# Overflow groups of 64 tokens, two to a tile, in an audio tower's tree feed-forward; the static residual moved next to its scatter

## The chip, the cores and the metric

The kernel runs on one core of one Trainium2 chip, in one launch. The metric is the device time of the launch in microseconds. The profile comes from one more execution, whose own time is given beside its span.

## What is computed

The input is four sequences of 750 x 128. A three-tap convolution of signs (64 features out) and a normalisation give h, 748 tokens a sequence, 2992 tokens in all. An attention of 8 heads, of which only the diagonal weight of each token is used, is added to h. Then comes the part that the change touches, a tree of 255 nodes with 128 leaves:

```python
current = zeros(T)                                  # T = 2992 tokens, all at the root
for _ in range(8):
    score = einsum('td,td->t', flat_x, w1s[current]) + b1s[current]
    choice = ((sign(score) + 1) / 2)
    current = current * 2 + choice + 1              # left or right child
path_weights = gelu(abs(logits))                    # 8 per token
for i in range(8):
    t_i = einsum('td,tdo->to', flat_x, w2s[nodes_i]) + b2s[nodes_i]
    out = out + t_i * path_weights[:, i]            # 64 x 64 matrix of each node on the path
h = h + out
```

Each token thus needs eight 64 x 64 matrices, and which eight depends on its leaf alone. How many tokens a leaf has is known only when the kernel runs.

## The kernel before

Five engines run their own instruction streams; semaphores order them. The work falls into two stages.

**Attention and routing (until about 360 us).** 16 units, each one pair of heads of one sequence, of 12 score tiles of 125 x 748. TensorE forms a tile (L964), VectorE takes its negated maxima (L1438), ScalarE the exponentials with their sums (L1238). Three PSUM tensors of 1024 columns take turns. Ahead of unit w, SP copies the high and low halves of q and k into stacks in SBUF: eight DMAs, four at L389 and four at L395, which unit w of TensorE waits for (`scores`, L961). SP issues all of these, the table loads and the zero fill in one order. The zero fill (L410) stands after the copies of w = 5: one DMA that writes a row of zeros, with a token number out of range, to every slot of the table `sorted_rows`, `F_TILES` x 128 slots of 130 floats. Later fills of the attention work compute each token's leaf, its rank in the leaf and its slot; GpSimd scatters the tokens' rows (normalised x, a one, h, token number) into their slots (L668).

**The tree (from 361.8 us).** A leaf has 32 static slots (`G`): tile k of 32 static tiles holds leaves 4k to 4k + 3. Tokens beyond 32 go to overflow groups of 32, four groups to a tile, at most `OVG` = 96 groups. A section is four tiles; SP loads its rows in one DMA (`load_rows`, six buffers `xs`), TensorE transposes them (`xs_T`, L1046), ScalarE copies that (`xs_copy`, L1303).

- Static tile: TensorE multiplies with fixed slices of the tables (L1066 to L1073); ScalarE computes the gates (L1310, L1312) and weighs the first four levels (L1321), VectorE the other four (L1730) and sums the eight levels (L1738) into one of `NO` = 12 buffers `yo`. GpSimd adds the residual (`residual`, L742) and scatters the 128 rows to the output (`rows_out`, L750). The loop issues residual k + 1 ahead of scatter k.
- Overflow tile: the leaf numbers of a tile's four groups are packed in one register, 7 bits each; of these TensorE computes the addresses. For each group four products with the group's 32 columns of the transposed rows as the stationary operand: 195, 130, 65 and 65 columns (L1096 to L1102), into one bank for each group (`OWN`); then one product of the whole tile with the root's matrix (L1108). ScalarE copies the four groups (L1342) and the root (L1344) to `yv` in SBUF, computes the gates; VectorE weighs all levels (L1727), sums (L1738) and adds the residual (L1744); GpSimd only scatters. Group g of the next tile waits until the copy of group g is out of its bank. `yv` and the weighted values have two buffers each.

The number of groups is loaded into a register on each engine. Each of the six sections is unrolled and stands in an `If` of its own, one behind the other. SP waits at the end for every scatter (L453, L457). SP's `load_rows(k)` from the seventh on waits until the tiles that had its buffer are scattered. VectorE's sum of tile k waits for the scatter of tile k - 12.

Of the kernel before, what the change touches and what calls it, by code (L numbers as in the profile page):

```python
# [11 lines left out]
DEPTH = 8  # L12
NODES = 2 ** DEPTH - 1
LEAVES = 2 ** (DEPTH - 1)
P = 128
# [24 lines left out]
G = 32  # L40
OVG = 96
STAT = LEAVES * G
SLOTS = STAT + OVG * G
ST_TILES, OV_TILES = STAT // P, OVG * G // P
# [18 lines left out]
def tower(nc, x, k_tok, bias, beta, mean, var, Wqkv, bqkv, W0, b0, w1s, b1s, w2s, b2s, rows, hbuf, out):  # L63
# [6 lines left out]
    with ctx:  # L70
# [114 lines left out]
        EARLY = 12  # L185
# [6 lines left out]
        def banks(k):  # L192

            return k + 4 * max(0, k - ST_TILES)
# [139 lines left out]
        def _(sp):  # L334
# [113 lines left out]
            for k in range(ST_TILES // 4, F_TILES // 4 - 1):  # L448
                with sp.If(groups > 4 * (4 * k - ST_TILES)):
                    load_rows(k + 1)  # L450
# [3 lines left out]
            for m in range(ST_TILES // 4, F_TILES // 4):  # L454
                with sp.If(groups > 4 * (4 * m - ST_TILES)):
                    for k in range(4 * m, 4 * m + 4):
                        sp.wait_ge(s_outr[k % NO], 16 * (k // NO + 1))  # L457

        @block.gpsimd
        def _(pool):  # L460
# [297 lines left out]
            for m in range(ST_TILES // 4, F_TILES // 4):  # L758
                with pool.If(groups > 4 * (4 * m - ST_TILES)):  # L759
                    for k in range(4 * m, 4 * m + 4):  # L760
                        rows_out(k)

        @block.tensor
        def _(pe):
# [312 lines left out]
            def load_leaves(k):  # L1077

                kk = k - ST_TILES
                return nc.tensor.value_load(lam4[0:1, kk:kk + 1], min_val=0, max_val=LEAVES ** 4 - 1)  # L1080

            def overflow_products(k, leaves):
# [4 lines left out]
                for g in range(4):  # L1087
                    if n:
                        pe.wait_ge(s_yv, 4 * (n - 1) + g + 1)
                    elif g % 2 == 0:  # L1090
                        bank_ready(ST_TILES + g // 2)
                    y = OWN[g][0:G]
                    xg = xk[:, G * g:G * (g + 1)]
                    own = leaves >> 7 * g if g else leaves
                    leaf = nc.tensor.snap(own & LEAVES - 1 if g < 3 else own)
# [15 lines left out]
            early = [load_leaves(k) for k in range(ST_TILES, ST_TILES + EARLY)]  # L1111
# [10 lines left out]
            for m in range(ST_TILES // 4, F_TILES // 4):  # L1122
                with pe.If(groups > 4 * (4 * m - ST_TILES)):
                    for k in range(4 * m, 4 * m + 4):
                        n = k - ST_TILES
                        overflow_products(k, early[n] if n < EARLY else load_leaves(k))
                        if k % 4 == 1 and k + 4 < F_TILES:
                            xs_T(m + 1)

        @block.scalar  # L1130
        def _(act):
# [202 lines left out]
            for m in range(ST_TILES // 4, F_TILES // 4):  # L1334
                with act.If(groups > 4 * (4 * m - ST_TILES)):
                    for k in range(4 * m, 4 * m + 4):
                        if k >= ST_TILES + 2:
                            act.wait_ge(s_wy, k - 1)
# [4 lines left out]
                        act.wait_ge(s_y, banks(k) + 5)  # L1343
                        sc_.copy(yv[:, k % 2, 0, 0, :], ROOT[k % 2][:, 0:E1]).then_inc(s_y0, 1)  # L1344
                        act.wait_ge(s_yv, 4 * (k - ST_TILES + 1))
                        act.wait_ge(s_y0, k - ST_TILES + 1)
                        gates(k, yv[:, k % 2])
                        if k % 4 == 1 and k + 4 < F_TILES:
                            xs_copy(m + 1)

        @block.vector
        def _(dve):
# [216 lines left out]
            def old_terms():  # L1569

                v.tensor_scalar(col[:, c_cap], col[:, c_grp], float(G), float(G + 1), ALU.mult, ALU.add)
# [6 lines left out]
            def group_slots(b):  # L1578
# [3 lines left out]
                link(v.tensor_scalar(col[:, c_new], z[:, 0:1], float(G), float(STAT + 1), ALU.mult, ALU.add))  # L1582
# [168 lines left out]
            for m in range(ST_TILES // 4, F_TILES // 4):  # L1751
                with dve.If(groups > 4 * (4 * m - ST_TILES)):
                    for k in range(4 * m, 4 * m + 4):
                        weigh(k)
                        sum_levels(k)
                        add_residual(k)
# [24 lines left out]
```

## Time and profile before

| | |
|---|---|
| median of 3 runs | 483.22 us (482.93 to 486.01) |
| the profiled execution | 478.25 us, span 476.4 us |
| busy, TensorE products | 357.5 us (75% of the span) |
| busy, VectorE | 344.1 us (72%) |
| busy, ScalarE | 325.3 us (68%) |
| busy, GpSimd | 276.7 us (58%) |
| instructions | 8299 |
| scatters to the output (L750) | 44, of 0.987 us |
| the zero fill (L410) | issued at 109.8 us |
| overflow weighting (L1727) | 12 times |
| granted TensorE clock, mean | 0.908 of 2.4 GHz |

The shares are means over all stages. What the change is worth is read in the stage that it touches, from the order of time on each engine there. In the rows below PE is TensorE's products, PEld its loads of the stationary operand, DVE VectorE, ACT ScalarE, POOL GpSimd and SP the engine that issues most DMAs; a q behind a name is the engine's sequencer. All positions are microseconds from the start of the span.

### The profile page before, as it was taken

What the parts mean: (1) busy time and instruction counts of PE and PEld (TensorE: products, weight loads), DVE (VectorE), ACT (ScalarE), POOL (GpSimd) and SP (SyncE); (2) the same over time, 40 slices, a digit from 0 to 9 for tenths busy, and PEclk for the clock granted to TensorE, in tenths of its full rate; (3) what the DMA queues carried; (4) which work ended last, traced back from release to release, by engine and by line L of the source; (5) the groups of instructions that cost most, each with busy time, mean ns of one, the idle gap of its engine ahead of it and who ended that gap; (6) DMA issues with size and microseconds to landing.
All of it is one profiled execution on the core that took longest, in us unless ns stands there. A gap on an engine that the chain in (4) does not pass through costs nothing. (4 is left out here: it accounts for less than half of the span.)

```text
span 476.4 us, 8299 instructions
## 1 busy us (share of the span) xinstructions
PE 357.5 (75%) x2588; PEld 251.8 (53%) x2588; DVE 344.1 (72%) x588; ACT 325.3 (68%) x832; POOL 276.7 (58%) x389
## 2 busy tenths in 40 slices
PE   1167898867898898778898668993313998989990
PEld 1144666645555564546664446662212776768880
DVE  0466869898888888997888997788720887864552
ACT  1455988788798898659797667678000887778771
POOL 4325762785868777676589661661462577863221
PEclk9997989999999999887999998795555999999997
DMA  4434342519969943031254120017915022200000
GB/s 94 128 79 118 97 100 56 122 35 197 217 144 180 158 98 97 17 81 34 65 117 113 26 73 1 1 42 113 119 36 150 12 56 58 51 12 11 7 8 8
DMA packets 58954, 37.28 MB, mean 78 GB/s; under 512 B 31661, under 2 KB 57607, under 8 KB 58906
## 3 DMA queue, kind: packets, MB, share of 16 engines
q1 hardware_dynamic: 54778, 33.81, 34.8%
q0 software_dynamic: 3328, 2.36, 2.0%
q10 hardware_dynamic: 800, 0.49, 0.5%
q8 instruction: 26, 0.43, 0.4%
q14 instruction: 22, 0.18, 0.1%
HBM read 11.42 MB, written 7.50 MB: 40 GB/s over the span
## 5 line engine op out<-in xcount | busy, mean ns | idle before, releaser
L1238 ACT ACTIVATE Z<-Z,nm 125x748 f32<-125x748 f32 x192 | 166.1, 870 | 64.4 <-DVE nm L1438 63.1
L1438 DVE TENSOR_REDUCE nm<-Z 125x1 f32<-125x748 f32 x192 | 175.7, 933 | 40.4 <-PE Z L964 34.3
L964 PE MATMUL Z<-pool_a 128*125 128x512 f16 (+1 forms) x768 | 168.2, 349 | 25.7 <-ACT Z L1238 22.0
L964 PEld LDWEIGHTS Z<-pool_a 128*125 128x125 f16 x768 | 92.2, 145 | 70.4 <-ACT Z L1238 43.1
L750 POOL DMA_INDIRECT out<-pre,va x44 | 43.4, 987 | 39.8 <-DVE pre L1744 31.7
L1738 DVE TENSOR_REDUCE pre<-va 128x64 f32<-128x512 f32 x44 | 45.5, 1035 | 9.1 <-ACT va L1321 4.7
L817 PE MATMUL Z<-xhT,wq 128*128 128x249 f16 (+1 forms) x192 | 33.1, 293 | 11.3 <-DVEq L1449 9.9
L1238 ACT ACTIVATION_READ_ACCUMULATOR Z<-Z,nm 125x1 f32 x192 | 40.9, 213 | 0.0
L668 POOL DMA_INDIRECT sorted_rows<-xrow,slot x24 | 29.4, 1223 | 18.7 <-DVE slot L1611 12.1
L628 POOL TENSOR_TENSOR va<-va 125x256 f32<-125x256 f32 (+2 forms) x54 | 29.6, 548 | 8.9 <-DVE va L1468 5.8
L1342 ACT COPY va<-Z 32x455 f32<-32x455 f32 x48 | 25.3, 526 | 8.6 <-PE Z L1102 5.6
L602 POOL CAST pool_a<-q 128x748 f16<-128x748 f32 x14 | 11.3, 808 | 33.7 <-ACT q L1180 24.9
L817 PEld LDWEIGHTS Z<-xhT,wq 128*128 128x128 f16 x192 | 19.0, 105 | 21.9 <-DVEq L1449 13.7
L604 POOL TENSOR_TENSOR pool_a<-q,pool_a 128x748 f16<-128x748 f32 x15 | 24.7, 1645 | 10.2 <-DVE pool_a L1395 9.1
L1321 ACT ACTIVATE va<-Z,gw 128x64 f32<-128x64 f32 x128 | 29.8, 315 | 1.2 <-DVE pre L1738 0.2
L1303 ACT COPY qk<-Z 65x512 f32<-65x512 f32 x12 | 7.0, 580 | 32.5 <-PE Z L1046 32.4
L832 PEld LDWEIGHTS Z<-sel,qk 128*125 128x125 f32 x192 | 26.3, 200 | 5.1 <-issue 0.8
L612 POOL TENSOR_TENSOR qk<-q,k 128x748 f32<-128x748 f32 x16 | 28.2, 1765 | 0.0
L1730 DVE TENSOR_TENSOR va<-Z,gw 128x256 f32<-128x256 f32 x32 | 13.3, 415 | 20.1 <-ACT gw L1312 19.2
L832 PE MATMUL Z<-sel,qk 128*125 128x2 f32 x192 | 25.6, 239 | 0.4 <-DVE pre L1532 0.4
L1066 PE MATMUL Z<-pool_a,qk 128*128 128x260 f32 x64 | 22.4, 429 | 3.4 <-ACT va L1321 2.5
L604 POOL TENSOR_TENSOR pool_a<-k,pool_a 128x748 f16<-128x748 f32 x15 | 24.0, 1602 | 1.1
(252 smaller groups left out, 642.4 us busy)
## 6 DMA issues: line engine op xcount, KB each, us to landing
pool_a<-pool_a SPq DMA_DIRECT2D x64, 187.0 KB, 3.3
pool_a<-pool_a SPq DMA_DIRECT2D x64, 93.5 KB, 2.2
sorted_rows<-zrow SPq DMA_DIRECT2D x1, 3640.0 KB, 21.3
va<-sorted_rows SPq DMA_DIRECT2D x12, 260.0 KB, 3.9
w<-in_L_ffn_w2s SPq DMA_DIRECT2D x1, 2048.0 KB
pre<-in_x SPq DMA_DIRECT2D x4, 375.0 KB
pool_a<-in_L_ffn_w2s SPq DMA_DIRECT2D x1, 1024.0 KB
out<-pre,va POOLq DMA_INDIRECT x44
```

Of the source, the lines that this page charges most:

```text
L604: gp.tensor_tensor(hl[:, c, n, 1, 0:N], (q32, k32)[n][:, c, 0:N], hl[:, c, n, 0, 0:N], ALU.subtract).then_inc(s_lo, 1)
L612: gp.tensor_tensor(qk[:, w % 3, 0:N], q32[:, w % 2, 0:N], k32[:, w % 2, 0:N], ALU.mult).then_inc(s_prod, 1)
L628: link(gp.tensor_tensor(pw[:, 0:n], pw[:, 0:n], pw[:, n:2 * n], ALU.add))
L668: gp.indirect_dma_start(rows, bass.IndirectOffsetOnAxis(slots[0:XP, t:t + 1].bitcast(u32), 0), xrow[0:XP, t, :], None, bounds_check=SLOTS - 1,
L750: gp.indirect_dma_start(outf, bass.IndirectOffsetOnAxis(ids.bitcast(u32), 0), yo[:, k % NO, :], None, bounds_check=T - 1, oob_is_err=False ...
L817: last = mm(z[:, PSUM_AT[c] % 512:PSUM_AT[c] % 512 + CLASS_N[c]], wq[:, a, g * H * D + j * P:g * H * D + (j + 1) * P], xhT[:, r0:r0 + CLAS ...
L832: last = mm(z[0:XP, t:t + NT + 1:NT], qk[:, w % 3, KST[t]:KST[t] + XP], sel[:], start=True, stop=True)
L964: last = mm(z[0:XP, c0:c1], kst[:, u % 3, a, hd, KST[t]:KST[t] + XP], qst[:, u % 3, hd, c0:c1], start=(a == 0), stop=(a == 1))
L1238: sc_.activation(z, z, ACT.Exp, bias=nm[0:XP, u % 4, i:i + 1], accum_out=sm[0:XP, u % 4, i:i + 1]).then_inc(s_exp, 1)
L1321: last = sc_.activation(wy[:, k % 2, n * D:(n + 1) * D], y[:, 0, n, 0:D], ACT.Copy, scale=gw[:, k % 4, n:n + 1])
L1438: v.tensor_reduce(nm[0:XP, u % 4, i:i + 1], Z[n % 3][0:XP, 0:N], X, ALU.max, negate=True).then_inc(s_max, 1)
L1738: v.tensor_reduce(yo[:, k % NO, :], wy[:, k % 2].rearrange("p (l o) -> p o l", o=D), X, ALU.add).then_inc(s_sl, 1)
```

## The change

Overflow groups hold 64 tokens, two to a tile; `OVG` stays 96, so there is room for 48 overflow tiles in 12 sections, and `F_TILES` goes from 56 to 80. A group's bank is used again by the tile after next instead of the next. One register serves two tiles. The sections' `If`s are nested instead of one behind the other (a helper, `sections`, used by all five engines). The counts of slots and groups are computed with the new size. In GpSimd's static loop, residual k is issued just ahead of scatter k. The core of it:

```diff
+G2 = 64
-SLOTS = STAT + OVG * G
-ST_TILES, OV_TILES = STAT // P, OVG * G // P
+SLOTS = STAT + OVG * G2
+ST_TILES, OV_TILES = STAT // P, OVG * G2 // P
...
-        EARLY = 12
+        EARLY = 8
...
-            return k + 4 * max(0, k - ST_TILES)
+            return k + 2 * max(0, k - ST_TILES)
+
+        def sections(engine, groups, work, m=ST_TILES // 4, end=F_TILES // 4):
+
+            if m < end:
+                with engine.If(groups > 2 * (4 * m - ST_TILES)):
+                    work(m)
+                    sections(engine, groups, work, m + 1, end)
...
-            residual(0)
             for k in range(ST_TILES):
-                if k + 1 < ST_TILES:
-                    residual(k + 1)
+                residual(k)
                 rows_out(k)
...
-                for g in range(4):
-                    if n:
-                        pe.wait_ge(s_yv, 4 * (n - 1) + g + 1)
-                    elif g % 2 == 0:
-                        bank_ready(ST_TILES + g // 2)
-                    y = OWN[g][0:G]
-                    xg = xk[:, G * g:G * (g + 1)]
+                for h in range(2):
+                    g = 2 * n + h
+                    if g >= 4:
+                        pe.wait_ge(s_yv, g - 3)
+                    elif h == 0:
+                        bank_ready(ST_TILES + n)
+                    y = OWN[g % 4][0:G2]
+                    xg = xk[:, G2 * h:G2 * (h + 1)]
...
-                        for g in range(4):
-                            act.wait_ge(s_y, banks(k) + g + 1)
-                            yw = yv[g * G:(g + 1) * G, k % 2].rearrange("p h l o -> p (h l o)")
-                            sc_.copy(yw[:, E1:DEPTH * E1], OWN[g][0:G, 0:7 * E1]).then_inc(s_yv, 1)
+                    for h in range(2):
+                        act.wait_ge(s_y, banks(k) + h + 1)
+                        yw = yv[h * G2:(h + 1) * G2, k % 2].rearrange("p h l o -> p (h l o)")
+                        sc_.copy(yw[:, E1:DEPTH * E1], OWN[(2 * n + h) % 4][0:G2, 0:7 * E1]).then_inc(s_yv, 1)
...
-                link(v.tensor_scalar(ogi[:, 0:1], col[:, c_new0], -1.0, float(G - 1), ALU.add, ALU.max))
-                link(v.tensor_scalar(ogi[:, 1:2], ogi[:, 0:1], 5, None, ALU.arith_shift_right))
+                link(v.tensor_scalar(ogi[:, 0:1], col[:, c_new0], float(G2 - G - 1), float(G2 - 1), ALU.add, ALU.max))
+                link(v.tensor_scalar(ogi[:, 1:2], ogi[:, 0:1], 6, None, ALU.arith_shift_right))
```

## Rows read from the trace of the kernel before

**Rows 1.** Busy time by engine in the overflow stage: us, busy (x count), granted clock

```profile
420.23:465.70 45.47, 45.06 (x420) 36.92 (x420) 24.97 (x38) 35.15 (x94) 15.65 (x18) 1.00 0.04 9
```

**Rows 2.** TensorE in order of time: start us, us, engine, line, operation

```profile
423.71 0.43 PE L1108 MATMUL Z<-pool_a,qk 128*128 128x65 f32 x2
...
457.60 0.44 PE L1108 MATMUL Z<-pool_a,qk 128*128 128x65 f32 x2
...
459.21 0.49 PE L1096 MATMUL Z<-pool_a,qk 128*32 x2
459.99 0.49 PE L1096 MATMUL Z<-pool_a,qk 128*32 x2
...
461.64 0.44 PE L1108 MATMUL Z<-pool_a,qk 128*128 128x65 f32 x2
...
465.24 0.44 PE L1108 MATMUL Z<-pool_a,qk 128*128 128x65 f32 x2
```

**Rows 3.** ScalarE and VectorE at the start of the overflow, in order of time

```profile
422.13 1.63 ACT L1342 COPY va<-Z 32x455 f32<-32x455 f32 x3
...
426.28 0.69 DVE L1727 TENSOR_TENSOR va<-va,gw 128x512 f32<-128x512 f32 x1 [2.38 <-ACT gw L1312]
...
428.14 0.22 DVE L1744 TENSOR_TENSOR pre<-pre,va 128x64 f32<-128x64 f32 x1
...
427.76 2.18 ACT L1342 COPY va<-Z 32x455 f32<-32x455 f32 x4 [1.52 <-PE Z L1108]
429.97 0.21 ACT L1344 COPY va<-Z 128x65 f32<-128x65 f32 x1
...
430.51 0.21 ACT L1312 ACTIVATE gw<-gw 128x8 f32<-128x8 f32 x1
```

**Rows 4.** Loads of 64 columns (ns min/median/max) and of 32 (busy us, mean ns)

```profile
L1070 PEld LDWEIGHTS Z<-pool_a,qk x128: 132/133/137, 368.5 to 419.4; 128*64 128x64 f32 x128
...
L1096 PEld LDWEIGHTS Z<-pool_a,qk 128*32 128x32 f32 x96 | 7.5, 109 | 2.3 <-issue 1.4
```

**Rows 5.** The end: last residual, last scatter, GpSimd's drain (duration ns min/median/max, start)

```profile
468.51 0.23 DVE L1744 TENSOR_TENSOR pre<-pre,va 128x64 f32<-128x64 f32 x1
...
469.53 0.97 POOL L750 DMA_INDIRECT out<-pre,va  x1 [2.60 <-DVE pre L1744]
...
L70 POOLq DRAIN  x1: 6349/6349/6349, 469.8 to 469.8; - x1
```

**Rows 6.** GpSimd's residuals and scatters in order of time

```profile
371.80 0.29 POOL L742 TENSOR_TENSOR pre<-pre,va 128x64 f32<-128x64 f32 x1 [10.90 <-DVE pre L1738]
...
413.53 0.34 POOL L742 TENSOR_TENSOR pre<-pre,va 128x64 f32<-128x64 f32 x1
...
415.05 0.31 POOL L742 TENSOR_TENSOR pre<-pre,va 128x64 f32<-128x64 f32 x1
...
426.18 0.97 POOL L750 DMA_INDIRECT out<-pre,va  x1 [0.30 <-issue]
```

**Rows 7.** DMA issues on the page: count, KB each, median us to landing

```profile
pool_a<-pool_a SPq DMA_DIRECT2D x64, 93.5 KB, 2.2
sorted_rows<-zrow SPq DMA_DIRECT2D x1, 3640.0 KB, 21.3
```

**Rows 8.** Line L389 from 108 to 128 us: issue ns, and landing us

```profile
L389 SPq DMA_DIRECT2D pool_a<-pool_a x4: 596/597/6347, 118.6 to 126.3; - x4
...
DMA to landing us min/median/max: 5.9/6.2/12.6
```

**Rows 9.** Line L395 from 128 to 150 us: issue ns, and landing us

```profile
L395 SPq DMA_DIRECT2D pool_a<-pool_a x7: 609/616/817, 127.6 to 143.7; - x7
...
DMA to landing us min/median/max: 6.2/6.3/7.3
```

**Rows 10.** TensorE's first products of unit 6 and of unit 7

```profile
142.29 0.85 PE L964 MATMUL Z<-pool_a 128*125 128x512 f16 x4
...
156.65 0.85 PE L964 MATMUL Z<-pool_a 128*125 128x512 f16 x4 [0.30 <-ACT Z L1238]
```

More of the change, by code:

```diff
@@ L447, in _, with written @@
             groups = sp.value_load(nact[0:1, 0:1], min_val=0, max_val=OVG)
-            for k in range(ST_TILES // 4, F_TILES // 4 - 1):
-                with sp.If(groups > 4 * (4 * k - ST_TILES)):
-                    load_rows(k + 1)
+            sections(sp, groups, lambda m: load_rows(m + 1), end=F_TILES // 4 - 1)
             for k in range(ST_TILES - NO, ST_TILES):
                 sp.wait_ge(s_outr[k % NO], 16 * (k // NO + 1))
[L454 to L457, printed above, removed]
+            def written(m):
+                for k in range(4 * m, 4 * m + 4):
+                    sp.wait_ge(s_outr[k % NO], 16 * (k // NO + 1))
+            sections(sp, groups, written)
         @block.gpsimd
@@ L751, in rows_out, with section_out @@
                                       bounds_check=T - 1, oob_is_err=False).then_inc(s_outr[k % NO], 16)
-            residual(0)
             for k in range(ST_TILES):
-                if k + 1 < ST_TILES:
-                    residual(k + 1)
+                residual(k)
                 rows_out(k)
[L758 to L761, printed above, removed]
+            def section_out(m):
+                for k in range(4 * m, 4 * m + 4):
+                    rows_out(k)
+            sections(pool, groups, section_out)
         @block.tensor
@@ L1086, in overflow_products @@
                 n = k - ST_TILES
[L1087 to L1095 removed]
+                for h in range(2):
[6 more added lines that the diff above has]
+                    xg = xk[:, G2 * h:G2 * (h + 1)]
+                    own = leaves >> 7 * (g % 4) if g % 4 else leaves
+                    leaf = nc.tensor.snap(own & LEAVES - 1 if g % 4 < 3 else own)
                     mm(y[:, 0:3 * E1], xg, wlow[:, bass.ds((leaf >> 4) * (4 * E1) + (T03 + 1) * E1, 3 * E1)],
@@ L1110, in _ @@
             pe.wait_ge(s_goff, 1)
-            early = [load_leaves(k) for k in range(ST_TILES, ST_TILES + EARLY)]
+            early = [load_leaves(j) for j in range(EARLY)]
             pe.wait_ge(s_tab, 16 * 2)
@@ L1121, in _, with section_products @@
             groups = pe.value_load(nact[0:1, 0:1], min_val=0, max_val=OVG)
[L1122 to L1128, printed above, removed]
+            def section_products(m):
+                for k in range(4 * m, 4 * m + 4):
+                    j = (k - ST_TILES) // 2
+                    if k % 2 == 0:
+                        leaves = early[j] if j < EARLY else load_leaves(j)
+                    overflow_products(k, leaves)
+                    if k % 4 == 1 and k + 4 < F_TILES:
+                        xs_T(m + 1)
+            sections(pe, groups, section_products)
         @block.scalar
@@ L1750, in _, with section_sums @@
             groups = dve.value_load(nact[0:1, 0:1], min_val=0, max_val=OVG)
[L1751 to L1756, printed above, removed]
+            def section_sums(m):
+                for k in range(4 * m, 4 * m + 4):
+                    weigh(k)
+                    sum_levels(k)
+                    add_residual(k)
+            sections(dve, groups, section_sums)
 _INS = ["x", "L0_tok_kernel", "L0_tok_bias", "L0_tok_beta", "L0_tok_moving_mean", "L0_tok_moving_var",
```

34 lines of the change are left out of this document (17 added, 17 removed).

## The prediction

> **What bounds the kernel now.** I read the stretches first, then the order of time by engine, then the end. The static tiles and the overflow tiles are stages of their own. In the second, 45.5 us long, TensorE is busy 45.06 us at the full granted clock, ScalarE 35.15, VectorE 24.97, GpSimd 15.65 [rows 1]: TensorE sets the pace. In order of time a root product follows the last at 3.60 us, at 4.04 us where four transposes stand between [rows 2]: four groups of 0.78 us and 0.48 us of root and change of shape. The 44 scatters of the table are 32 static tiles and 12 overflow tiles, so the inputs give 33 to 48 groups of 32. From the last root (465.24) to the last scatter's start (469.53) is a chain of 4.29 us; scatter and GpSimd's drain fill the rest of the 476.4 us [rows 2, 5].
>
> **How many tiles come after.** From the reference's inputs I counted tokens by leaf: 29 leaves have more than 32 tokens, 3 of these more than 96 (99, 100, 138). That is 45 groups of 32 (12 tiles, as the trace has it), and 26 + 3 x 2 = 32 groups of 64: 16 tiles, four sections. 32 is the last number that four sections hold; a 33rd opens a fifth.
>
> **TensorE's chain.** A group streams the same 455 columns whatever its tokens, so I keep 0.78 us. A tile is 3.60 - 2 x 0.78 = 2.04 us, plus 0.44 per four tiles for the transposes. The stage begins as now at 420.23. Its first root comes 3.48 us after that, 0.85 us a group; with two groups less it moves from 423.71 to 422.0 [rows 2]. Last root: 422.0 + 15 x 2.04 + 4 x 0.44 = 454.4; plus 4.29: last scatter starts at 458.7. The stationary operand grows from 32 to 64 columns: loads of those widths take 109 and 133 ns [rows 4]. The price of the 24 ns is zero if they stay under the running product and 8 x 24 = 0.19 us a group if not (eight loads a group); below zero isn't possible. I take zero, since loads are busy 36.92 us of the 45.47 beside products that are busy 45.06 [rows 1]: they overlap.
>
> The Trainium skill (TensorE: Matmul & The Clock Gate, LDWEIGHTS) says a load takes its columns divided by 1.2 GHz, so 53 ns for 64 against 27 for 32; by it the unhidden price would be 0.21 us a group (an estimate from that page), near the rows' 0.19.
>
> **VectorE's chain.** Weigh, sum and residual take 426.28 to 428.36; with the hand-over 2.12 us a tile. Today the first weigh waits for four ScalarE copies and begins at 426.28. ScalarE starts copying at 422.13; two copies of 0.545, then root copy, Abs and Gelu (0.75 from 429.97 to 430.72) give 424.0, and a hand-over 424.1 [rows 3]. Last residual ends at 424.1 + 16 x 2.12 = 458.0, its scatter starts 0.79 us later: 458.8. ScalarE's own tile is 2 x 0.545 + 0.75 = 1.84 us and a transposed copy every fourth: third.
>
> **GpSimd's chain, the second edit.** Today residual k+1 stands between residual k and scatter k, so GpSimd's sequencer prepares the scatter meanwhile: in a busy stretch a tile costs 1.52 us (413.53 to 415.05) [rows 6]. After, scatter k waits for its own residual. No row shows that wait on GpSimd; the nearest is the overflow scatter behind VectorE's residual, 0.79 us from end to start [rows 5]. Bounds: 1.52 us (nothing lost) and 0.34 + 0.79 + 0.97 + 0.02 = 2.12 us. I take 2.12, because in its row the same instruction waits for the same kind of addition, only on another engine. The first scatter starts at 371.80 + 0.29 + 0.79 = 372.9; the 32nd at 372.9 + 31 x 2.12 = 438.6, against 426.18 today [rows 6]. GpSimd thus enters the overflow 12 us late, but its scatters there need only 1.27 us (0.97, and 0.30 of issue between them where work is queued [rows 6]): last start 439.6 + 0.30 + 15 x 1.27 = 459.0. The lag holds up nobody before that: VectorE's sum waits for the scatter 12 tiles back (that of tile 19 starts at 372.9 + 19 x 2.12 = 413, over 7 us before the sum of tile 31, which comes after TensorE has left the static tiles at 420.23). SP's last load of rows waits for tile 27 (430), wanted near 420.23 + 13 x 2.15 = 448.
>
> So three chains end within 0.3 us (458.7, 458.8, 459.0). Two stages of equal pace, coupled through two tiles of banks, lose something to bunched transposes: I allow 0.9 us: 459.9.
>
> **What moves earlier.** The row table grows from 7168 to 10240 rows, so the zero fill, one DMA of 3640 KB that lands after 21.3 us, grows by 3/7. A small copy lands in 2.2 us, which I take for the fixed part: + (21.3 - 2.2) x 3/7 = 8.2 us [rows 7]. The stack copies of unit 6 are issued behind the fill on SP's queue: of the first four, from 118.6 on, one holds SP for 6.35 us and one lands only after 12.6 us, at 131.2 [rows 8]; the fill, issued at 109.8 (table above), lands at 131.1. The last four are issued up to 128.9 and land after 6.2 to 7.3 us [rows 9], so by 135.1 to 136.2. Plus 8.2: 143.3 to 144.4, and TensorE begins unit 6 at 142.29 [rows 10]: a stall of 1.0 to 2.1 us; I take 1.5. SP then runs 8.2 us late. Unit 7's last copy goes out at 143.7 [rows 9]; plus 8.2 that is 151.9, and 4.7 us are left to land until the unit begins at 156.65 [rows 10], against 2.2 for a copy of half its size: no stall, by little. Ends of this term: 0, and 4 us if unit 7 waits too.
>
> The Trainium skill (DMA: Bandwidth & Descriptors, Queues, rings and completion order) says each DMA engine consumes a queue's descriptors in ring order. By that rule the stall comes; if the copies could pass the fill there would be none and the sum 1.5 us lower. The 131.2 above agrees with the rule.
>
> Costed at nothing: the register loads ahead of the static tiles (there are fewer); the branch at a section's start (the roots at such a place keep their pace); the jump out after the last section, under GpSimd's drain of 6.35 us from 469.8 on [rows 5]; the other arithmetic on counts, which changes constants only.
>
> **Sum.** Scatter start 469.53 - 459.9 = 9.6 us gained, less 1.5: 8.1 us. The profiled execution took 478.25 (span 476.4 and 1.85 around it): 470.1. The median of the runs shown lies 5.0 us above it, and I keep that offset: 475.1.
>
> **Rivals.**
> - GpSimd sets the end by more. Every 0.1 us beyond 2.12 adds 3.1 us to its chain. With 2.25: 463.0, gain 5.0 us, 478. For it: no slack in this chain and the price is borrowed. Chance 0.15.
> - The other side, same mechanism: from 2.41 us a tile GpSimd's chain and the stall together put the last scatter at 469.5 again; at 2.55 it is 4.3 us slower: 487.5. Against it: it needs 0.3 to 0.4 us more between release and scatter than the 0.79 of the row. Chance 0.04.
> - The weight loads show: 2 x 0.19 us on 16 tiles, 6.1 us: gain 2.0, 481. Chance 0.07.
> - SP's lateness does not stay within unit 6: units 7 and 8 stall too, 4 us instead of 1.5: gain 5.6, 477.6. Chance 0.10.
> - A 33rd group (a leaf with 32 tokens gets one more by rounding): a fifth section, 4 x 2.15 = 8.6 us: gain -0.5, 483.7. Chance 0.04.
> - The end doesn't follow, because the drain after the last scatter grows with GpSimd's back-to-back scatters by 5 us or so: gain 3, 480. Against it: none of the rows shows such a backlog, so the chance is small, 0.05.
>
> **From cases to numbers.** Forecast 0.55, its own range 472.5 to 477. A run can tell from no change about 1%, 4.8 us. Over 1% faster: forecast 0.55, GpSimd 0.11, SP 0.09, weights and drain 0.03: 0.78. Within 1%: 0.15. Slower: 0.07, of it 0.04 GpSimd, the rest a fifth section with a longer stall. The range runs from 471.5 (no stall and no coupling loss give 472.7, and the three runs shown differ by more than the 1.2 below that) to 481, the weight loads; beyond lie a fifth section and GpSimd past 2.41.
>
> **What would show it.** Weighting 16 times; roots 2.04 us apart; TensorE's group at 0.78 us; GpSimd's scatter 0.79 us behind its residual and a tile in 2.12; the 32nd scatter near 438.6 plus the stall, and GpSimd without waits until the last tiles; fill landing after 29 to 30 us and TensorE waiting for a stack copy near 142. Wrong it would be made by a fifth section, or by a GpSimd tile well above 2.12.

## The result: slower by 1%, where 1.7% faster was forecast

The changed kernel took 484.69 us (median of 20 runs, 477.03 to 490.92), the kernel before, run beside it, 478.03 us (20 runs, 473.93 to 486.01). The ratio is 1.0095, 95% interval 1.0063 to 1.0126: slower, outside the forecast of 475.1 us and its range. The ratio compares the faster runs of each kernel only and leaves out those over 1.5% above the kernel's fastest, so it is smaller than the 1.014 between the two medians. The profiled execution took 477.03 us (span 475.3), the fastest of the twenty and 1.2 us under the profiled one of before, so its trace shows the changes stage by stage, but not all that the median lost.

**Leaf stage (the static and overflow tiles, from TensorE's first transpose on).** These groups of the profile after (by line and shape: busy us, mean ns, then idle time before and its releasers) answer to [rows 2 to 4]:

```profile
L1742 DVE TENSOR_TENSOR va<-va,gw 128x512 f32<-128x512 f32 x16 | 11.3, 708 | 6.2 <-ACT gw L1324 3.4 <-issue 2.7
L1104 PE MATMUL Z<-pool_a,qk 128*64 x64 | 16.6, 342 | 0.4 <-issue 0.4
L1104 PEld LDWEIGHTS Z<-pool_a,qk 128*64 128x64 f32 x64 | 6.2, 136 | 2.0 <-issue 1.2
```

Sixteen overflow tiles, as counted, and TensorE hardly idles ahead of its groups. Its root products in order of time (start, us):

```profile
431.78 0.44 PE L1116 MATMUL Z<-pool_a,qk 128*128 128x65 f32 x2
433.86 0.44 PE L1116 MATMUL Z<-pool_a,qk 128*128 128x65 f32 x2
...
453.44 0.44 PE L1116 MATMUL Z<-pool_a,qk 128*128 128x65 f32 x2
456.05 0.44 PE L1116 MATMUL Z<-pool_a,qk 128*128 128x65 f32 x2
459.07 0.44 PE L1116 MATMUL Z<-pool_a,qk 128*128 128x65 f32 x2
```

They stand 2.08 us apart, 2.5 to 2.6 where transposes stand between, and 3.0 at the very end, beside scatters that stand back to back. The last root is at 459.07 where it was at 465.24 [rows 2], yet the last scatter starts later than before. GpSimd in order of time, first static tiles, then the end:

```profile
379.88 0.29 POOL L750 TENSOR_TENSOR pre<-pre,va 128x64 f32<-128x64 f32 x1 [10.96 <-DVE pre L1753]
381.04 1.04 POOL L758 DMA_INDIRECT out<-pre,va  x1 [0.87 <-POOL pre L750]
...
445.64 0.99 POOL L758 DMA_INDIRECT out<-pre,va  x1 [0.79 <-POOL pre L750]
446.66 0.34 POOL L750 TENSOR_TENSOR pre<-pre,va 128x64 f32<-128x64 f32 x1
447.79 0.99 POOL L758 DMA_INDIRECT out<-pre,va  x1 [0.79 <-DVE pre L1759]
449.09 1.45 POOL L758 DMA_INDIRECT out<-pre,va  x1 [0.30 <-DVE pre L1759]
...
468.79 0.97 POOL L758 DMA_INDIRECT out<-pre,va  x1 [0.30 <-issue]
470.06 0.97 POOL L758 DMA_INDIRECT out<-pre,va  x1 [0.30 <-issue]
```

From 381.04 to 470.06 GpSimd never idles for want of work: 2.15 us for each static tile (445.64 to 447.79), then scatter behind scatter, 1.27 us each where nothing lengthens it. VectorE is done with the last tile 3 us before:

```profile
466.82 0.23 DVE L1759 TENSOR_TENSOR pre<-pre,va 128x64 f32<-128x64 f32 x1
```

So GpSimd sets the end, with 89.0 us from first to last scatter.

**Ahead of it: attention and routing, which the expectations below call the tree stage.** The first scatter starts at 381.04, 8.1 us after the 372.9 that the forecast had without the fill, and all of it is lost before the leaf stage begins: TensorE's first transpose of the row table starts at 373.04, before the change at 364.96. SyncE's DMA issues (start, us in issue, count), what TensorE waited for stack copies over the whole run (us in total, times, longest), the products that waited so with the first product of unit 7, and the fill on the page:

```profile
108.82 0.60 SPq L418 DMA_DIRECT2D sorted_rows<-zrow  x1
117.64 20.26 SPq L397 DMA_DIRECT2D pool_a<-pool_a  x4
137.94 2.59 SPq L403 DMA_DIRECT2D pool_a<-pool_a  x4
```

```profile
PE Z L972 <- DMA pool_a<-pool_a: 8.3, 2, 5.2
```

```profile
38.41 3.97 PE L972 MATMUL Z<-pool_a 128*125 128x512 f16 x12 [3.10 <-DMA pool_a<-pool_a]
...
146.57 1.48 PE L972 MATMUL Z<-pool_a 128*125 128x512 f16 x4 [5.16 <-DMA pool_a<-pool_a]
...
163.68 0.85 PE L972 MATMUL Z<-pool_a 128*125 128x512 f16 x4 [0.31 <-ACT Z L1250]
```

```profile
sorted_rows<-zrow SPq DMA_DIRECT2D x1, 5200.0 KB, 33.6
```

The four issues behind the fill hold SyncE for 20.26 us, with one of them at 6.35 before [rows 8]; TensorE stands 5.16 us, starting unit 6 at 146.57 where it had been 142.29 [rows 10]. Of the 8.3 us in total the other 3.10 lie at 38.41 us, 70 us ahead of the fill, where the kernel before stands 2.65; they have nothing to do with it. Then comes what the forecast had no term for. The same ten microseconds in both traces, after and then before (us; busy (x count) of TensorE, its loads, VectorE, ScalarE, GpSimd; granted clock, DMA share, GB/s):

```profile
145.00:155.00 10.00, 8.43 (x33) 6.53 (x34) 4.34 (x6) 3.02 (x7) 3.15 (x8) 0.50 0.61 139
```

```profile
145.00:155.00 10.00, 8.19 (x50) 5.02 (x49) 8.07 (x13) 9.32 (x24) 8.42 (x14) 1.00 1.31 167
```

In this stretch, behind the stall, the granted clock is half (1.2 GHz of 2.4), and TensorE needs 8.43 us for 33 products instead of 8.19 for 50. From the first product of unit 6 to that of unit 7 it takes 17.11 us (146.57 to 163.68), where before it took 14.36 [rows 10]: 2.75 us is the price of the half clock. Unit 7 starts with no wait for a stack, as before. Just ahead of the stall this run had been 0.95 us ahead of the one before (a tile of unit 5 at 137.58 against 138.53), so the stall moved TensorE by 5.2 us and the half clock by 2.8: 7.0 us late at unit 7. The last 1.0 us of the 8.1 came later.

### The profile page after: what moved, and what is told of

It is laid out like the page before. It is cut to its first block, busy times and chain, and to the rows that moved or that the text cites. A ratio compares the mean times of both kernels' runs of the same rounds, so it can differ in the third digit from the quotient of the medians.

```text
span 475.3 us, 8000 instructions
## 1 busy us (share of the span) xinstructions
PE 345.3 (73%) x2472; PEld 244.2 (51%) x2472; DVE 352.4 (74%) x600; ACT 320.8 (67%) x829; POOL 283.3 (60%) x393
## 4 chain that ended last, share of the span: by engine, by line
DVE 29%; PE 19%; issue 16%; ACT 13%; POOL 11%; DMA 7%; SPq 2%; POOLq 1%; DVEq 0%; ACTq 0%
DVE nm L1453 11%; PE Z L972 9%; ACT Z L1250 8%; POOL out L758 7%; DMA pre<-in_x 3%; DMA pool_a<-pool_a 2%; DVE va L1483 2%; POOL pre L750 2%; DVE pre L1567 2%; ACT q L1192 2%; DVE pre L1753 2%; PE Z L840 1%; ACT k L1192 1%; PE Z L825 1%; SPq L397 1%
## 5 line engine op out<-in xcount | busy, mean ns | idle before, releaser
L972 PEld LDWEIGHTS Z<-pool_a 128*125 128x125 f16 x768 | 90.3, 143 | 78.8 <-ACT Z L1250 47.3
L758 POOL DMA_INDIRECT out<-pre,va x48 | 49.2, 1025 | 30.4 <-POOL pre L750 24.7
L1753 DVE TENSOR_REDUCE pre<-va 128x64 f32<-128x512 f32 x48 | 49.8, 1038 | 6.8 <-ACT va L1333 2.0
L1192 ACT ACTIVATE q<-Z,bq 128x249 f32<-128x249 f32 (+1 forms) x48 | 20.7, 474 | 3.5 <-PE Z L825 3.4
L1355 ACT COPY va<-Z 64x455 f32<-64x455 f32 x32 | 17.0, 531 | 9.0 <-PE Z L1110 5.9
## 6 DMA issues: line engine op xcount, KB each, us to landing
sorted_rows<-zrow SPq DMA_DIRECT2D x1, 5200.0 KB, 33.6
```

The costliest lines, as they stand in the source:

```text
L758: gp.indirect_dma_start(outf, bass.IndirectOffsetOnAxis(ids.bitcast(u32), 0), yo[:, k % NO, :], None, bounds_check=T - 1, oob_is_err=False ...
L972: last = mm(z[0:XP, c0:c1], kst[:, u % 3, a, hd, KST[t]:KST[t] + XP], qst[:, u % 3, hd, c0:c1], start=(a == 0), stop=(a == 1))
L1192: last = sc_.activation(dst[:, CLASS_AT[c]:CLASS_AT[c] + CLASS_N[c]], z[:, PSUM_AT[c] % 512:PSUM_AT[c] % 512 + CLASS_N[c]], ACT.Identity, ...
L1753: v.tensor_reduce(yo[:, k % NO, :], wy[:, k % 2].rearrange("p (l o) -> p o l", o=D), X, ALU.add).then_inc(s_sl, 1)
```

## The experiments

Eighteen runs in five groups; kernels of a group ran on one chip, beside the kernel before. Ratios are of that one, with 95% intervals, so ratios of one group compare best. The chip of the result above is called the first chip. A backlog is a row of scatters that are all ready to go, so that GpSimd issues them one right behind the other; a hole is a stretch in which VectorE stands.

### Fill and order, one at a time (chip 12, before 480.21 us)

Small table (it also halves the unrolled sections; the split fills of the next group keep them all): the changed kernel with

```
-OVG = 96
+OVG = 48
```

> The changed kernel with room for 48 groups instead of 96: table and zero fill go back to 7168 rows, everything else of the change stays. Theory F (the longer fill, in front of the stack copies on SP's queue, costs the time; its price was sized 1.5 us and is 8 us or more with the half clock after it): TensorE has no long wait near 142 us, the fill lands after about 21 us, rows for the tree arrive near 362 us as before the change, the last scatter starts near 462, and the kernel is 7 us (1.5%) faster than before: ratio 0.985. Rival R (GpSimd's order is the whole loss): the time stays that of the changed kernel, ratio 1.01. Rival C (more unrolled code and nested branches slow the stages): half the sections are gone, so some gain too, but the attention's stretch from 100 to 180 us stays as slow as in the changed kernel.

Old order of residual and scatter in the changed kernel:

```
             for k in range(ST_TILES):
-                residual(k)
+                if k + 1 < ST_TILES:
+                    residual(k + 1)
                 rows_out(k)
```

(with residual(0) ahead of the loop)

> The changed kernel with GpSimd's old order, residual k + 1 ahead of scatter k. Theory F: still the long fill, so ratio to before near 1.005; GpSimd's static tile is 1.5 us again, and the last scatter follows VectorE's last residual by 0.79 us, 2 to 3 us earlier than in the changed kernel. Rival R: all of the loss goes, ratio 0.985 or less.

The kernel before with a row table and a fill of 80 tiles, of which it uses 56 (the core of the edit):

```
-                                 zrow[:].unsqueeze(1).to_broadcast([P, F_TILES, RW])).then_inc(s_fill, 16)
+                                 zrow[:].unsqueeze(1).to_broadcast([P, FILL_TILES, RW])).then_inc(s_fill, 16)
```

> The kernel before with nothing changed but the table and the fill, which take 10240 rows. Theory F: fill lands after about 33 us, TensorE waits 5 to 8 us for stack copies, its clock falls to half behind that wait, rows for the tree arrive some 8 us later, and the kernel is 8 to 14 us slower than before: ratio 1.017 to 1.03. The prediction's own sizing of that fill, 1.5 us, gives 1.003. Rivals R and C: 1.00.

Small table and old order together:

> Both undone: room for 48 groups, so the short fill, and GpSimd's old order; what is left is the two groups of 64 a tile. Theory F with the prediction's chains: the last scatter starts 9 to 10 us earlier than before (near 460), ratio 0.98, and 2 us less than with the small table alone. If the two edits' costs are not separate (GpSimd no bound), it equals the small table alone.

| kernel | ratio | first transpose | first to last scatter |
|---|---|---|---|
| small table | 0.9897 (0.9864 to 0.9931) | 365.57 | 95.3 us |
| old order | 0.9951 (0.9913 to 0.9988) | 372.02 | 89.7 us |
| before, large fill | 1.0191 (1.0152 to 1.0230) | 373.94 | 97.4 us |
| small table, old order | 0.9817 (0.9766 to 0.9867) | 364.49 | 90.9 us |

The large fill alone costs the kernel before 1.9%, some 9 us; between the two kernels with groups of 64 and the old order it costs 1.3%, 6.4 us (0.9951 against 0.9817). The trace shows what the changed kernel's shows (waits, of which 5.6 us behind the fill and the rest at 37.7 us; then SyncE's issues):

```profile
PE Z L966 <- DMA pool_a<-pool_a: 8.3, 2, 5.6
```

```profile
119.52 19.93 SPq L391 DMA_DIRECT2D pool_a<-pool_a  x4
```

With neither the large fill nor the new order, groups of 64 gain 1.8%, 8.8 us (6.4 to 11.2), where the forecast had 9.6 for the leaf stage. By the traces of this chip it is less: from the first transpose to the last scatter the kernel before with the large fill takes 106.5 us, the two with groups of 64 and the old order 98.6 and 99.6. The new order costs 0.8% with the small table (0.9897 against 0.9817). The old order with the large fill landed at 0.9951, between the two outcomes expected for it. The trace of the small table had a hole: VectorE waits 12.85 us for ScalarE's gates while GpSimd scatters without a pause.

```profile
459.80 0.69 DVE L1742 TENSOR_TENSOR va<-va,gw 128x512 f32<-128x512 f32 x1 [12.85 <-ACT gw L1324]
```

### Where the fill costs, and the order elsewhere (chip 0, before 479.24 us)

The kernel before with the new order alone:

> The kernel before with one edit: GpSimd adds tile k's residual just ahead of scatter k, where it had added that of tile k + 1. Overflow tiles and fill stay. Theory (order cheap by itself): the twelve old overflow tiles leave GpSimd idle between two of their scatters, so the later static scatters catch up there: 0.998 to 1.004 of before, about 480.5 us on this chip, with last scatter within 0.5 us of where it was. Rival 1 (order dear wherever it stands): the same price as between the two versions of the small table, 0.8%, or as between the two versions of the large one, 1.4%: 484 to 487 us. Rival 2 (order gains): under 0.995.

The fill in seven pieces, with the old order and with the new:

```
-                if w == 5:
...
+                if w in FILL_AT:        # (5, 6, 8, 9, 10, 11, 12)
+                    t0 = 12 * FILL_AT.index(w)
+                    t1 = min(t0 + 12, F_TILES)
+                    sp.dma_start(rows.rearrange("(t p) c -> p t c", p=P)[:, t0:t1, :],
+                                 zrow[:].unsqueeze(1).to_broadcast([P, t1 - t0, RW])).then_inc(s_fill, 16)
```

> The changed kernel with the residual of k + 1 ahead of scatter k again, and the zero fill, of the same size, given out in seven pieces of twelve tiles over seven units instead of in one. Theory (what costs is one long fill ahead of the stacks of the next tree unit on SyncE's queue): the pieces pass beside the tree stage, PE's wait for the stacks is back to under 3 us, no stretch at half clock near 147 us, and the time is that of the small table with the old order: 0.982 of before (0.978 to 0.988), 469 to 475 us. Rival (what costs is the bytes, wherever they go): as the large fill with the old order, 0.995 of before.

> The changed kernel with the fill in seven pieces alone; GpSimd keeps the new order of residual and scatter. Theory: the fill's price (some 9 us) goes and that of the order stays: 0.990 of before (0.985 to 0.995), 473 to 478 us, and the last section shows GpSimd's scatters back to back with TensorE and VectorE waiting beside them. Rival (the order's price was an effect of timing with the small table): as e6_split_old, 0.982.

The fill in one piece, from ScalarE's queue:

```
+                    if (u, i) == (4, 0):
+                        act.dma_start(rows.rearrange("(t p) c -> p t c", p=P),
+                                      zrow[:].unsqueeze(1).to_broadcast([P, F_TILES, RW])).then_inc(s_fill, 16)
```

> The changed kernel with its large fill in one piece, given out by ScalarE at its fourth unit instead of by SyncE. Theory A (order on SyncE's queue: the stacks' DMAs wait for room behind the fill's descriptors): the L397 issues on SyncE are under 10 us again, PE's wait for the stacks is under 3 us, and the time is some 0.990 to 0.998 of before. Theory B (the fill's packets share the 16 DMA engines with the stacks, whoever gives it out): PE still waits 5 us or more and falls to half clock: 1.005 to 1.012. Rival C: ScalarE itself stands 10 us or more in the issue of the fill or of what follows, and TensorE waits for it: above 1.012.

Measured: before with the new order 1.0012 (0.9977 to 1.0048); split fill, old order 0.9724 (0.9680 to 0.9769), 466.43 us; split fill, new order 0.9921 (0.9886 to 0.9955); fill from ScalarE 0.9936 (0.9897 to 0.9975). The rows of the last one, the fill on the page and SyncE's issues:

```profile
sorted_rows<-zrow ACTq DMA_DIRECT2D x1, 5200.0 KB, 35.0
```

```profile
119.47 3.33 SPq L397 DMA_DIRECT2D pool_a<-pool_a  x4
124.02 2.79 SPq L403 DMA_DIRECT2D pool_a<-pool_a  x4
...
128.21 17.33 SPq L383 DMA_DIRECT2D xrow<-h_rows  x12
```

The fill is as long as ever and overlaps the stack copies, yet those leave SyncE in 3.33 us instead of 20.26, and TensorE never waits for one behind the fill (its 2.6 us in total lie at 37.7 us). So it is the place behind the fill on one queue that delays the stacks, not the bytes. (The twelve copies of L383 take 17.33 us here, 5.03 in the split kernel; nobody is late for it.) The Trainium skill (DMA: Bandwidth & Descriptors, Queues, rings and completion order) has SyncE and ScalarE on rings of their own, each consumed in order; the 3.33 against 20.26 agrees. In the split kernels the same issues take 2.73 us. The split fill with the new order and the fill from ScalarE sit where "order on the queue" put them, the split one with the old order below it. The new order costs 2.0% here (0.9921 against 0.9724), and nothing in the kernel before, though that trace has a hole of 9.35 us too (below: what the order gives back).

### Does the backlog of scatters starve the others? (chip 11, before 480.88 us)

In four traces with a backlog (small table; split fill; ScalarE's fill; before with the new order) VectorE stood 12.85, 6.45, 9.99 and 9.35 us in one place beside scatters 0.30 us apart, and each hole ended 0.1 to 3.0 us after the end of the last of them. I took the spacing of 0.30 us between scatters for the cause, and put an instruction between them:

```
                 else:
+                    gp.tensor_tensor(spare[:, k % 24, :], half[:], half[:], ALU.add)
                     pool.wait_ge(s_yov, k - ST_TILES + 1)
```

> The kernel with the split fill and the new order of residual and scatter (0.9921 of before), with one small tensor_tensor of 128x64 to a spare buffer added on GpSimd ahead of each overflow scatter, so that two scatters in a row never stand 0.30 us apart. Theory (scatters back to back starve the other engines): the backlog is worked off at some 1.5 us a tile instead of 1.27, with TensorE, ScalarE and VectorE at their 2.08 us pace beside it; no wait of VectorE over 2.5 us in the overflow sections; 0.980 to 0.988 of before, though GpSimd has more to do. Rival (the backlog itself or the section's entry stops the others, not the spacing): waits of 3 us and more stay, and with the extra instructions the time is 0.992 or above.

> The kernel before with its own fill (56 tiles) given out in five pieces over five units. Theory (SyncE's queue is what a fill costs): the 21 us fill of the kernel before costs some 2 to 4 us of its own already, as its L389 issues stand 8 us: 0.990 to 0.996 of before, 475 to 478 us. Rival (a 21 us fill is hidden): 0.998 to 1.003.

> The kernel with the split fill and the old order of residual and scatter (0.9724 of before), with the same spacing instruction ahead of each overflow scatter. Theory (back-to-back scatters starve): only three scatters stood back to back there, with waits of 0.9 and 1.5 us in it; these shrink, and the last scatter starts up to 0.3 us later after its sum: 0.970 to 0.975, no change that can be measured. Rival: the added instruction costs 0.3 us at each of 16 tiles on the path: 0.980 or more.

> The changed kernel as it stands (1.0095 of before) with the spacing instruction ahead of each overflow scatter as its only edit. Theory: TensorE's overflow tiles keep 2.08 us apart through the last section (they fell to 3.0), scatters take 0.97 to 1.27 instead of up to 1.45; GpSimd works off its backlog at 1.5 us instead of 1.27 and ends within 1 us of VectorE: 0.998 to 1.006. Rival (spacing is not the cause): 1.010 or more, as GpSimd, which ends last, gets 16 x 0.3 us more.

Measured: split, new order, spaced 0.9834 (0.9796 to 0.9871); before with its own fill in five pieces 0.9983 (0.9942 to 1.0023), so the 21 us fill was hidden; split, old order, spaced 0.9779 (0.9719 to 0.9839), which with the same kernel unspaced at 0.9724 can't be told apart; changed kernel, spaced 0.9906 (0.9871 to 0.9942), below both outcomes expected for it. In the two with a spaced backlog VectorE waited 1.52 us at most in the overflow. That looked like proof, but the unspaced kernels had run on other chips, so the next group put them side by side.

### The same question on one chip (chip 15, before 469.90 us)

> The changed kernel once more, unchanged, beside the kernel before and the other runs of this call on one chip. Expected again at 1.0095 of before (1.005 to 1.014).

> The changed kernel with the spacing instruction ahead of each overflow scatter as its only edit, once more, beside the changed kernel itself. Before it stood at 0.9906 of the kernel before on another chip than the changed kernel's 1.0095. Theory A (the spacing is worth what the two numbers say): 0.985 to 0.995 here, some 1.9% under the changed kernel beside it. Theory B (part of it was chance in the tree stage, where this run's SyncE stood 17.3 us in the stacks' issues and TensorE did not fall to half clock): 0.996 to 1.003, some 0.9% under it, as between the two kernels with the split fill.

And a backlog made on purpose in the kernel with split fill and old order, GpSimd holding back the last twelve static scatters, without and with the spacing:

```
-            for k in range(ST_TILES):
-                if k + 1 < ST_TILES:
-                    residual(k + 1)
-                rows_out(k)
+            for k in range(HOLD):       # HOLD = ST_TILES - NO = 20
+                residual(k + 1)
+                rows_out(k)
+            for k in range(HOLD + 1, ST_TILES):
+                residual(k)
+            for k in range(HOLD, ST_TILES):
+                rows_out(k)
```

> The kernel with the split fill and the old order (0.9724 of before) with a backlog made on purpose: GpSimd adds the residuals of the last twelve static tiles first and only then gives out their twelve scatters, one right behind the other, while the overflow tiles begin. Theory (scatters back to back starve TensorE, ScalarE and VectorE): VectorE waits 5 us or more at one of the first overflow tiles, as it did with the small table and the new order: 0.980 to 0.990 of before. Rival (a backlog alone is harmless while buffers are there): 0.970 to 0.978.

> The same backlog made on purpose, with a 128x64 tensor_tensor to a spare buffer ahead of each of the twelve scatters and of each overflow scatter: 28 instructions more on GpSimd. Theory (spacing, not backlog): VectorE's waits at the overflow tiles are under 2.5 us, and the time is below that of the backlog without the spacing by 0.5% or more. Rival (backlog as such): as that kernel or slower.

Measured: changed kernel 1.0016 (0.9976 to 1.0055), with the spacing 1.0196 (1.0161 to 1.0230); backlog 0.9804 (0.9769 to 0.9840), spaced 1.0042 (1.0018 to 1.0066). The changed kernel was expected at 1.005 to 1.014 again and isn't slower here. The spacing was to gain 0.5% to 1.9% and costs 1.8% and 2.4%. The backlog's ratio is at the edge of what starvation would give, but its trace shows none: no wait of TensorE or ScalarE over 0.5 us in the overflow, with 28 scatters back to back. The changed kernel here, VectorE's end and then GpSimd's:

```profile
452.78 0.69 DVE L1742 TENSOR_TENSOR va<-va,gw 128x512 f32<-128x512 f32 x1
454.62 0.26 DVE L1759 TENSOR_TENSOR pre<-pre,va 128x64 f32<-128x64 f32 x1
```

```profile
461.00 0.97 POOL L758 DMA_INDIRECT out<-pre,va  x1 [0.30 <-issue]
462.27 0.97 POOL L758 DMA_INDIRECT out<-pre,va  x1 [0.30 <-issue]
```

Undisturbed, VectorE is ready at 454.88 and GpSimd's last scatter starts 7.4 us later. First to last scatter is 87.8 us; with the spacing 92.5, 4.6 more, for 16 instructions that move a scatter from 1.27 to 1.49 us (3.5) and little else. GpSimd's own work is the bound, plainly. The fill cost less too. It landed after 30.0 us, TensorE waited for the stacks behind it as long as the forecast had it, and the first transpose came at 366.37:

```profile
143.62 0.82 PE L972 MATMUL Z<-pool_a 128*125 128x512 f16 x4 [1.44 <-DMA pool_a<-pool_a]
```

Across all traces with the large fill on SyncE's queue the stall goes with the landing: 30.0, 30.1 and 30.4 us give 1.4, 1.8 and 1.9 us (chips 15, 11, 15), and 32.5, 32.6 and 33.6 give 3.8, 5.6 and 5.2 (chip 12 twice, the first chip).

### The same backlog on one more chip (chip 14, before 481.28 us)

> The kernel with the backlog made on purpose once more, beside the same kernel without it. In its first run 28 scatters stood back to back and no other engine waited over 2.1 us in the overflow sections, so the theory that back-to-back scatters starve the others by themselves has fallen on that chip. Theory A (they never do; what had looked like it came from elsewhere): on this chip too there are no waits over 2.5 us in the overflow sections, and the time is 1% or more under that of the kernel beside it, 0.960 to 0.972 of before, as its last scatter follows its first by 80 us where that kernel needs 86. Theory B (they do on some chips or in some executions): waits of 3 us and more of VectorE in the overflow sections, and 0.975 or above.

> The kernel with the split fill and the old order of residual and scatter once more, beside the kernel before and the one with the backlog. It stood at 0.9724 (0.968 to 0.977). Theory: it repeats within 0.967 to 0.981 on any chip, since nothing in it depends on a backlog; rival (the chip decides as much as the change, as for the changed kernel, which stood at 1.0095 on one chip and 1.0016 on another): outside of that.

Measured: 1.0032 (0.9998 to 1.0066) with the backlog, 0.9782 (0.9737 to 0.9827) without. The same program that had its last scatter 80.2 us behind the first on chip 15 needs 101.5 here. VectorE, GpSimd, TensorE in order of time:

```profile
430.95 0.69 DVE L1750 TENSOR_TENSOR va<-va,gw 128x512 f32<-128x512 f32 x1 [2.46 <-ACT gw L1332]
...
445.70 0.69 DVE L1750 TENSOR_TENSOR va<-va,gw 128x512 f32<-128x512 f32 x1 [12.68 <-ACT gw L1332]
```

```profile
437.16 0.97 POOL L761 DMA_INDIRECT out<-pre,va  x1 [0.30 <-issue]
438.43 0.97 POOL L761 DMA_INDIRECT out<-pre,va  x1 [0.30 <-issue]
439.71 0.97 POOL L761 DMA_INDIRECT out<-pre,va  x1 [0.30 <-issue]
440.99 0.97 POOL L761 DMA_INDIRECT out<-pre,va  x1 [0.30 <-issue]
448.57 0.97 POOL L761 DMA_INDIRECT out<-pre,va  x1 [6.61 <-DVE pre L1767]
```

```profile
438.72 0.27 PE L1116 MATMUL Z<-pool_a,qk 128*64 x1 [0.52 <-issue]
440.12 0.27 PE L1116 MATMUL Z<-pool_a,qk 128*64 x1 [1.14 <-issue]
441.53 0.27 PE L1118 MATMUL Z<-w,qk 128*64 x1 [1.14 <-issue]
443.62 0.27 PE L1118 MATMUL Z<-w,qk 128*64 x1 [1.81 <-issue]
445.11 0.91 PE L1112 MATMUL Z<-pool_a,qk 128*64 x2 [1.22 <-ACT va L1363]
```

While scatters stand 0.30 us apart, TensorE gets a single product out every 1.4 us, waiting for nothing that the profile shows, and the pace is back at 445.11, 3.15 us after the end of the last scatter of the backlog. So theory B held: on chip 14 the backlog, beside its twin without one, makes the hole. Unspaced backlogs come with holes on chips 0, 12 and 14 and not on chip 15; on the first chip the changed kernel's slows TensorE's roots to 3.0 us and no more. That it is the spacing of 0.30 us, and not the backlog as such, no pair of runs on one chip shows. The kernel without a backlog repeats its gain, 0.9724 and 0.9782, and beats the kernel before on both chips: split fill, groups of 64, old order.

### One more reading across all traces

From TensorE's first transpose to VectorE's first weighing of an overflow tile, the static stage, there are two sorts:

| | us |
|---|---|
| new order, nine traces, chips 0, 11, 12, 15 and the first | 53.1 to 53.9, once 55.0 |
| old order, chip 15 (two traces) | 52.9, 53.4 |
| old order, the other chips (nine traces) | 58.8 to 63.4 |

One of each sort, the changed kernel, the backlog on chip 15, and the kernel with the split fill on chip 14:

```profile
426.29 0.87 DVE L1742 TENSOR_TENSOR va<-va,gw 128x512 f32<-128x512 f32 x1 [0.20 <-ACT gw L1324]
```

```profile
416.00 0.75 DVE L1750 TENSOR_TENSOR va<-va,gw 128x512 f32<-128x512 f32 x1 [0.20 <-ACT gw L1332]
```

```profile
433.05 0.69 DVE L1746 TENSOR_TENSOR va<-va,gw 128x512 f32<-128x512 f32 x1 [3.16 <-ACT gw L1328]
```

Their first transposes are at 373.04, 362.65 and 370.18. In the old order GpSimd issues a scatter every 1.5 us without a pause, and on all chips but 15 the other engines take 5 to 10 us longer beside it; in the new order each scatter waits 0.79 us, and they lose nothing. So the new order seems to give TensorE and VectorE back 5 to 10 us in the static stage and takes them again: by GpSimd's longer chain, which ends last, and by the stops when its backlog is worked off. The kernel before with the new order shows both, 55.0 us for the 61.3 of the first chip and then 9.35 us in one hole: 1.0012. On chip 15 the old order loses nothing to begin with, and the kernel before takes 469.90 us there. That dense scatters are the cause in the static stage as well is my reading of these traces; no run varied their density there alone. By it chip 11, where the old order took 63.1 and 63.3 us, is a chip that they hurt, and the spaced backlogs that ran there without a hole speak for the spacing after all; the unspaced twin was not run on that chip.

## Why the prediction was wrong, step by step

- **Tiles and TensorE's chain: right.** 16 tiles, four sections; 2.08 us from root to root against 2.04. The load of 64 columns took 136 ns and stayed hidden: the roots stand 0.04 us further apart than forecast. By the load rule of the Trainium skill (TensorE: Matmul & The Clock Gate, LDWEIGHTS) loads that don't hide would have made that 0.42 us, an estimate from that page; its 53 ns for 64 columns isn't what the trace shows.
- **The leaf stage's gain: near, and with the old order only.** 9.6 us forecast; 8.8 us by ratio with small table and old order, 6.9 and 7.9 by the traces of that chip. In the changed kernel's own trace first transpose to last scatter takes 97.0 us instead of 104.6: 7.5. The ratio's interval holds all of these, so that 8.8 lies near 9.6 is weaker support than it looks.
- **GpSimd's chain: mechanism right, size 3 us short.** 2.12 us a static tile forecast, 2.15 measured; from first to last scatter 86.1 us forecast (372.9 to 459.0), 89.0 measured and 87.8 on chip 15. The "three chains within 0.3 us" was the flaw in it: this one had no slack at all, the new order makes it the bound, and it costs 0.8 to 2.0% where I had nothing. A gain that I hadn't seen either stood against it: TensorE's first overflow root came 52.0 us after the first transpose where it had been 58.8 [rows 2] and 57.0 was forecast, and GpSimd's chain hid all of it. On the overflow tiles four scatters of 1.41 to 1.45 us, each beside a VectorE product of L1742, make up part of it.
- **The fill: the step that failed.** "A stall of 1.0 to 2.1 us; I take 1.5", ends 0 and 4. Measured: first transpose 8.1 us later; by ratio 9 us in the kernel before and 6.4 with groups of 64 and the old order. Two things were wrong in the term. First, the landing: the extra bytes were extrapolated at 19.1 us for 3640 KB, giving 29.5 us; the fill landed after 33.6, and the stall was 5.16 us. On chip 15, where it landed after 30.0, the stall was 1.44 us, inside the forecast, so the working from landing to stall was sound. Second, the price of a stall was taken to be its length: behind it came 10 us at half clock, worth 2.8 us, for which the sum had no term. The mechanism, order on SyncE's queue, was right.
- **From trace to median.** Last scatter 461.4 forecast, 470.06 measured: 8.7 us, of which the fill, ahead of the tree, 6.6 and the leaf stage 2.1. The end behind it is 1.6 us shorter (5.24 us to the span's end, 6.87 before). The profiled execution is therefore 6.9 us over the forecast's 470.1, and the median stands 7.7 us above it where I had kept 5.0: together 9.6. The three runs shown of before were high; its median of 20 is 478.03.
- **Rivals.** GpSimd setting the end (0.15) came in its mechanism, with 2.15 us a tile instead of 2.25. SyncE's lateness spreading beyond unit 6 (0.10) did not come in this trace: units 7 and 8 wait for no stack (on chip 11, in the changed kernel with the spacing, one later unit waited 1.12 us, at 176.09). The fill's loss came at unit 6, by a longer stall and by the clock, for which there was no rival. The two losses together take the whole gain, a combination that I gave no chance of its own.

Open: by what way dense scatters hold up the other engines, and why not on chip 15; whether that is all of the kernel before's 469.90 us there against 478 to 481 elsewhere; and what spreads the changed kernel over 477.03 to 490.92 us. Its mean granted clock runs from 0.904 in the fastest of the twenty to 0.858 in the slowest, but only the fastest has a trace, so where the clock is lost in the others isn't known. Two traces of one program show such a loss: with the split fill and the old order the first transpose came at 363.65 on chip 0, where the clock was at 0.98 from 60 to 140 us, and at 370.18 on chip 14, where it was at 0.91.

## What to carry to other kernels

Price a long DMA by what is issued behind it on the same queue, give it out in pieces, and count for a stall of TensorE its length and the stretch at half clock that can follow (here 5.2 and 2.8 us). When three chains come out within 1 us of each other, look for the one with no slack: a new order of instructions that lengthens it is not free, and what it frees elsewhere stays hidden. Compare two versions on one chip only: here a spacing that seemed to gain 1.9% between two chips cost 1.8% on one.

## What the runs showed of the hardware

- Behind a fill of 5200 KB from one row of 520 bytes, four issues on SyncE took 17.3 to 20.3 us; behind pieces of 780 KB 2.7 us; with the fill on ScalarE's queue 3.3 us.
- That fill landed after 30.0 to 33.6 us from SyncE's queue, depending on the run and the chip, and after 35.0 from ScalarE's.
- A scatter starts 0.79 us after the addition that releases it, whether GpSimd's own or VectorE's; with that addition one tile ahead, 0.17 us after the instruction in front, and with nothing in between 0.30.
- A GpSimd scatter of 0.97 us took 1.41 to 1.52 in all thirteen cases in which a 128x512 VectorE product of two SBUF inputs had started 0.04 to 0.12 us ahead of it; where it started first, or within 0.02 us behind the product, it stayed at 0.97 to 0.99. An addition of 0.31 us on GpSimd takes up to 0.84 beside VectorE.
- On chips 0, 12 and 14 TensorE's issue fell, in an unspaced backlog, to as little as one product in 1.4 us; on chip 15 its roots kept their 2.08 us beside 17 and 28 scatters back to back.
- One program can differ by 21 us between two chips in one stage (80.2 and 101.5 us from first to last scatter).
